# A second buffer for the input block, its squares computed a stage ahead, and two weight slots for three

## The reference

```
u = einsum('ntc,hc->nth', x, W_in)          # x: the normed input
gate, xh = split(u, 2)                      # 1536 channels each
xh = causal_depthwise_conv(xh, conv_w, conv_b)          # 4 taps
forget, inp = split(einsum('nth,gh->ntg', xh, W_gates) + b_gates, 2)
alpha = exp(-8.0 * softplus(forget_base) * sigmoid(forget))
beta = sqrt(1.0 - alpha ** 2 + 1e-06)
h = scan(alpha, beta * sigmoid(inp) * xh)   # h[t] = alpha[t] h[t-1] + xs[t]
out = einsum('nth,dh->ntd', gelu(gate) * h, W_out)
...
x = x + layernorm(attn(layernorm(x)))
x = x + layernorm(ffn(layernorm(x)))        # 8 experts, top 2, and a shared one
```

## Time and profile before

| | us |
|---|---|
| runs shown, lower and higher | 5487.73 and 5763.81 |
| their median | 5625.77 |
| profiled execution, its own time | 5491.87 |
| its span, core 4 | 5490.3 |
| spans of the 8 cores | 5464.4 to 5490.3 |
| attention half (from the start to about) | 2064 |

### The profile page before, as it was taken

One profiled execution on the slowest core, in us unless ns is written; L12 is line 12 of the kernel. 1 busy time (PEld: TensorE's weight loads), 2 busy tenths in 40 slices (PEclk: granted clock), 3 DMA queues, 4 the chain that ended last, 5 costly groups with the idle time before them and its releaser, 6 DMA issues.

```text
span 5490.3 us, 51919 instructions; the slowest of 8 cores (5464.4 to 5490.3 us)
## 1 busy us (share of the span) xinstructions
PE 3922.1 (71%) x15984; PEld 1604.2 (29%) x16304; DVE 2466.9 (45%) x4064; ACT 1187.5 (22%) x1715; POOL 632.0 (12%) x1186
## 2 busy tenths in 40 slices
PE   5566566656464753888888898873688888888883
PEld 1122222212121211333333333330233333333331
DVE  2433433333424245544445544446444554444545
ACT  1342242304132230221111211110111121111220
POOL 1010101111111110111111111110011111111110
PEclk9787788778787875999999999995899999999996
DMA  4454454444353530343333343330233334333341
GB/s 71 61 85 64 64 81 67 66 60 68 47 86 45 81 52 16 56 73 64 62 62 59 62 71 62 62 62 31 39 62 62 59 63 70 63 62 62 58 72 41
DMA packets 179676, 336.65 MB, mean 61 GB/s; under 512 B 19424, under 2 KB 39920, under 8 KB 179280
## 3 DMA queue, kind: packets, MB, share of 16 engines
q0 software_dynamic: 175248, 324.92, 37.5%
q1 hardware_dynamic: 4160, 8.39, 0.4%
HBM read 649.41 MB, written 8.39 MB: 120 GB/s over the span
## 4 chain that ended last, share of the span: by engine, by line
PE 62%; DVE 15%; ACT 11%; DMA 6%; issue 5%; DVEq 1%; ACTq 0%; POOL 0%; another core or an unknown queue 0%; POOLq 0%
PE pb L163 62%; ACT bufA L816 4%; DMA wi<-wi_xh 2%; DMA wi<-wi_gate 2%; DVE sh L469 1%; DVE sa L451 1%; DMA sxbf<-xin 1%; ACT L447 1%; ACT sla L447 1%; ACT L503 1%; DVE sxnbf L366 1%; DVE ssqbf L361 1%; DVE sa L454 1%; DVE st L463 1%; DVE st L466 1%
## 5 line engine op out<-in xcount | busy, mean ns | idle before, releaser
L163 PE MATMUL pb<-xn,wq 128*128 128x512 bf16 x9030 | 2027.7, 379 | 278.5 <-ACT bufA L816 268.3
L163 PEld LDWEIGHTS pb<-xn,wq 128*128 128x128 bf16 x9216 | 881.9, 98 | 1430.0 <-issue 411.4
L163 PE MATMUL pb<-sxh,wg 128*128 128x512 bf16 x2256 | 589.2, 421 | 366.3 <-ACT ssf L503 337.6
L163 PE MATMUL pb<-a_s,w2s 128*128 128x512 bf16 x2258 | 544.5, 401 | 127.6 <-DVE a_s L871 124.9
L816 ACT ACTIVATE bufA<-pb,c_b1g 128x512 f32<-128x512 f32 x256 | 175.9, 687 | 1678.4 <-PE pb L163 1678.4
L821 DVE SCALAR_TENSOR_TENSOR bufA<-pb,c_b3g,bufA 128x512 f32<-128x512 f32 x256 | 192.2, 751 | 674.8 <-ACT bufA L816 674.8
L163 PEld LDWEIGHTS pb<-sxh,wg 128*128 128x128 bf16 x2304 | 237.6, 106 | 717.7 <-issue 519.2
L163 PE MATMUL pb<-sxnbf,wi 128*128 128x512 bf16 x1128 | 303.3, 408 | 145.8 <-DVE sxnbf L366 71.1
L163 PEld LDWEIGHTS pb<-a_s,w2s 128*128 128x128 bf16 x2304 | 231.7, 102 | 432.4 <-issue 196.3
L850 DVE TENSOR_TENSOR bufA<-bufA,bufC 128x512 f32<-128x512 f32 x288 | 199.5, 693 | 241.3 <-ACT bufC L845 241.3
L845 ACT ACTIVATE bufC<-bufA 128x512 f32<-128x512 f32 x288 | 181.2, 629 | 467.3 <-DVE bufA L840 467.2
(11 more groups left out here) (143 smaller groups left out, 2926.0 us busy)
## 6 DMA issues: line engine op xcount, KB each, us to landing
wg<-wgates POOLq DMA_DIRECT2D x192, 384.0 KB, 5.7
wq<-w1g POOLq DMA_DIRECT2D x128, 256.0 KB, 4.1
wq<-w3g POOLq DMA_DIRECT2D x128, 256.0 KB, 4.8
wq<-w1l POOLq DMA_DIRECT2D x128, 256.0 KB, 6.2
wq<-w3l POOLq DMA_DIRECT2D x128, 256.0 KB, 7.0
w2s<-w POOLq DMA_DIRECT2D x128, 256.0 KB, 5.1
wi<-wi_xh POOLq DMA_DIRECT2D x96, 256.0 KB, 4.8
wi<-wi_gate POOLq DMA_DIRECT2D x48, 256.0 KB, 4.8
```

The source lines that it names most:

```text
L163: t.matmul(o, l, r, start=s1, stop=s2),
```

## The change

The input block and its squares get two buffers each, `sxbf2` and `ssqbf2`, used in turn by even and odd stages. Stage 0 loads and squares its own block ahead of the loop. In each stage but the last, behind the normalisation, the next block's load is put into GpSimd's list, ahead of the stage's `wi` loads, and its eight squares into VectorE's list, ahead of the roll and the evictions. The load into a buffer waits for what last read that buffer, two stages back from its own stage. Room is made by dropping `sla`, `st1` and `sh`: the middle part now works in place in `ssf`, `ssi` and `sa2`, and the closing norm in `sao` in place of `ssqbf`. The `wi` stream has two slots where it had three. Counts of instructions of each kind stay as they were.

```diff
-            sxbf = asb("sxbf", [128, NC_D, ST], BF16)
+            sxbf2 = asb("sxbf2", [128, 2, NC_D, ST], BF16)
...
-            ssqbf = asb("ssqbf", [128, NC_D, ST], BF16)
+            ssqbf2 = asb("ssqbf2", [128, 2, NC_D, ST], BF16)
...
-            sla = asb("sla", [128, 2, ST], F32)
...
-            st1 = asb("st1", [128, 2, ST], F32)
-            sh = asb("sh", [128, 2, ST], F32)
...
-            wi = WStream([asb(f"wi{j}", [128, NC_D, 128], BF16) for j in range(3)], "wi", "wi")
+            wi = WStream([asb(f"wi{j}", [128, NC_D, 128], BF16) for j in range(2)], "wi", "wi")
...
+            pre = {}
+            pre[0] = {"xld": g_dma(sxbf2[:, 0], d_x[:, :, 0:ST], sem="x0", tag="x0"),
+                      "xsem": "x0"}
+            sq_v0 = []
+            for c in range(NC_D):
+                v_op(lambda v, c=c: v.tensor_tensor(out=ssqbf2[:, 0, c, :],
...
+            pre[0]["sq_v"] = sq_v0
...
-                lw = [guard["sxbf"]] if "sxbf" in guard else []
-                xld = g_dma(sxbf[:], d_x[:, :, T0:T0 + ST], waits=lw, sem="x",
-                            tag=f"x{st}")
...
-                sqw = [guard["ssqbf"]] if "ssqbf" in guard else []
-                sq_v = []
-                for c in range(NC_D):
...
+                sxbf = sxbf2[:, par]
+                ssqbf = ssqbf2[:, par]
+
+                xld = pre[st]["xld"]
+                sq_v = pre[st]["sq_v"]
+                xw = [(pre[st]["xsem"], xld), ("c", wc)]
...
-                guard["ssqbf"] = ("v", S.n["v"])
                 xn_done = ("v", S.n["v"])
+                guard[("ssqbf", par)] = xn_done
                 if not main:
-                    guard["sxbf"] = xn_done
+                    guard[("sxbf", par)] = xn_done
...
+                if st + 1 < _nst:
+                    np_ = (st + 1) % 2
+                    lw = [g for g in (guard.get(("sxbf", np_)),) if g]
+                    nxld = g_dma(sxbf2[:, np_], d_x[:, :, T0 + ST:T0 + 2 * ST],
+                                 waits=lw, sem=f"x{np_}", tag=f"x{st + 1}")
+                    sqw = [g for g in (guard.get(("ssqbf", np_)),) if g]
+                    nsq = []
+                    for c in range(NC_D):
+                        v_op(lambda v, c=c, np_=np_: v.tensor_tensor(
+                                out=ssqbf2[:, np_, c, :],
...
+                             waits=([(f"x{np_}", nxld)] + sqw) if c == 0 else [],
+                             tag=f"sq{st + 1}")
+                        nsq.append([("v", S.n["v"])])
+                    pre[st + 1] = {"xld": nxld, "sq_v": nsq, "xsem": f"x{np_}"}
...
-                            out=sla[:, pp, :], in0=ssf[:, pp, :],
+                            out=ssf[:, pp, :], in0=ssf[:, pp, :],
...
-                            out=sla[:, pp, :], in_=sla[:, pp, :], func=AF.Exp),
+                            out=ssf[:, pp, :], in_=ssf[:, pp, :], func=AF.Exp),
...
-                            out=sa2[:, pp, :], in0=sla[:, pp, :], in1=sla[:, pp, :],
+                            out=sa2[:, pp, :], in0=ssf[:, pp, :], in1=ssf[:, pp, :],
...
-                            out=st1[:, pp, :], in0=sa2[:, pp, :], in1=ssi[:, pp, :],
+                            out=ssi[:, pp, :], in0=sa2[:, pp, :], in1=ssi[:, pp, :],
...
-                            out=sh[:, pp, :], data0=sla[:, pp, :], data1=st1[:, pp, :],
+                            out=sa2[:, pp, :], data0=ssf[:, pp, :], data1=ssi[:, pp, :],
...
-                                in1=sh[:, pp, :], op=OP.mult),
+                                in1=sa2[:, pp, :], op=OP.mult),
...
+                guard[("ssqbf", par)] = ("t", stats_done)
...
-                            out=ssqbf[:, c, :], in0=sao[:, c, :], in1=pb[6][:, :],
+                            out=sao[:, c, :], in0=sao[:, c, :], in1=pb[6][:, :],
...
-                            out=sao[:, c, :], in0=ssqbf[:, c, :], in1=pb[7][:, :],
+                            out=sao[:, c, :], in0=sao[:, c, :], in1=pb[7][:, :],
...
-                guard["ssqbf"] = ("v", S.n["v"])
...
-                guard["sxbf"] = ("v", S.n["v"])
+                guard[("sxbf", par)] = ("v", S.n["v"])
```

More of the change, by code:

```diff
@@ L333, in build_nc @@
             _nst = int(_os.environ.get("KDBG_NST", NST))
+            pre = {}
[4 more added lines that the diff above has]
+                v_op(lambda v, c=c: v.tensor_tensor(out=ssqbf2[:, 0, c, :],
+                                                    in0=sxbf2[:, 0, c, :],
+                                                    in1=sxbf2[:, 0, c, :], op=OP.mult),
+                     waits=([("x0", pre[0]["xld"])]) if c == 0 else [],
+                     tag="sq0")
+                sq_v0.append([("v", S.n["v"])])
+            pre[0]["sq_v"] = sq_v0
             for st in range(_nst):
@@ L360, in build_nc @@
                 for c in range(NC_D):
-                    v_op(lambda v, c=c: v.tensor_tensor(
+                    v_op(lambda v, c=c, sxbf=sxbf, ssqbf=ssqbf: v.tensor_tensor(
                             out=ssqbf[:, c, :], in0=sxbf[:, c, :],
@@ L365, in build_nc @@
                          tag=f"xna{st}")
-                    v_op(lambda v, c=c: v.tensor_tensor(
+                    v_op(lambda v, c=c, ssqbf=ssqbf: v.tensor_tensor(
                             out=sxnbf[:, c, :], in0=ssqbf[:, c, :],
@@ L370, in build_nc @@
                     xn_v[c] = ("v", S.n["v"])
-                guard["ssqbf"] = ("v", S.n["v"])
                 xn_done = ("v", S.n["v"])
+                guard[("ssqbf", par)] = xn_done
                 if not main:
-                    guard["sxbf"] = xn_done
+                    guard[("sxbf", par)] = xn_done
                 bank_guard[6] = xn_done
                 bank_guard[7] = xn_done
+                if st + 1 < _nst:
[8 more added lines that the diff above has]
+                                out=ssqbf2[:, np_, c, :],
+                                in0=sxbf2[:, np_, c, :],
+                                in1=sxbf2[:, np_, c, :], op=OP.mult),
+                             waits=([(f"x{np_}", nxld)] + sqw) if c == 0 else [],
+                             tag=f"sq{st + 1}")
+                        nsq.append([("v", S.n["v"])])
+                    pre[st + 1] = {"xld": nxld, "sq_v": nsq, "xsem": f"x{np_}"}
                 if st > 0:
@@ L463, in midtail @@
                     v_op(lambda v, pp=pp: v.tensor_tensor(
-                            out=st1[:, pp, :], in0=sa2[:, pp, :], in1=ssi[:, pp, :],
+                            out=ssi[:, pp, :], in0=sa2[:, pp, :], in1=ssi[:, pp, :],
                             op=OP.mult), waits=[beta_done], tag=f"bsi{st}")
                     v_op(lambda v, pp=pp, mi=mi: v.tensor_tensor(
-                            out=st1[:, pp, :], in0=st1[:, pp, :], in1=sxh[:, mi, :],
+                            out=ssi[:, pp, :], in0=ssi[:, pp, :], in1=sxh[:, mi, :],
                             op=OP.mult), tag=f"xs{st}")
                     v_op(lambda v, pp=pp, mi=mi: v.tensor_tensor_scan(
-                            out=sh[:, pp, :], data0=sla[:, pp, :], data1=st1[:, pp, :],
+                            out=sa2[:, pp, :], data0=ssf[:, pp, :], data1=ssi[:, pp, :],
                             initial=hcol[:, mi:mi + 1], op0=OP.mult, op1=OP.add),
@@ L473, in midtail @@
                     v_op(lambda v, pp=pp, mi=mi: v.tensor_copy(
-                            out=hcol[:, mi:mi + 1], in_=sh[:, pp, ST - 1:ST]),
+                            out=hcol[:, mi:mi + 1], in_=sa2[:, pp, ST - 1:ST]),
                          tag=f"hc{st}")
@@ L562, in build_nc @@
                         ao_a = ("a", S.n["a"])
-                        v_op(lambda v, m=m, b=b: v.tensor_tensor(
+                        v_op(lambda v, m=m, b=b, ssqbf=ssqbf: v.tensor_tensor(
                                 out=ssqbf[:, m, :], in0=sxnbf[:, m, :],
@@ L578, in build_nc @@
                     v_op(lambda v, c=c: v.tensor_tensor(
-                            out=sao[:, c, :], in0=ssqbf[:, c, :], in1=pb[7][:, :],
+                            out=sao[:, c, :], in0=sao[:, c, :], in1=pb[7][:, :],
                             op=OP.subtract), tag=f"x1b{st}")
-                    v_op(lambda v, c=c, Tm=Tm: v.tensor_tensor(
+                    v_op(lambda v, c=c, Tm=Tm, sxbf=sxbf: v.tensor_tensor(
                             out=x1[:, c, Tm:Tm + ST], in0=sao[:, c, :],
                             in1=sxbf[:, c, :], op=OP.add), tag=f"x1c{st}")
-                guard["ssqbf"] = ("v", S.n["v"])
                 guard["sao"] = ("v", S.n["v"])
-                guard["sxbf"] = ("v", S.n["v"])
+                guard[("sxbf", par)] = ("v", S.n["v"])
                 bank_guard[6] = ("v", S.n["v"])
```

## The result

The changed kernel is slower by one per cent: the ratio of its time to that of the kernel before is 1.0097, with a 95% interval of 1.0081 to 1.0112. Its executions took 5536.3 to 5544.0 us, those of before 5483.9 to 5491.7. The forecast was 5547; the profiled execution took 5544.4.

A forecast was written before the change was run, and what follows sets the result against it. The prediction took the attention half to be bound by waits for the input block and wi reloads, not matmuls. From 5491.87 us, plus 132.4 for loops, minus 77.3 for entries, it forecast 5547 us, range 5505 to 5620.

The forecast's parts named there:

- Entries of stages 1 to 7: Start of stages 1 to 7: row statistics no longer wait for the input load or its squares; gain 77.3 us.
- Loops: Projection loops with two wi slots: 21.8 us longer with both projections, 11.3 with one; 132.4 us in all.
- The landing time: wi loads in the projection loop: 4.1 us from issue to landing, with 3.7 and 4.84 as ends.
- The 0.9 us for a last load that meets those for `wg`: End of each projection loop: the last wi load meets the wg loads and adds 0.9 us.
- one group per loop go at the lower clock: Projection loop: one matmul group takes 3.4 us for 1.9 at the lower clock, adding 1.5 us per loop.
- rival (a): Projection loop: TensorE falls to the lower clock; 72 us more, giving 5619; chance 0.14.
- the verdict behind the sum: Whole kernel: sum 1.0% slower, but measurement taken to tell only about 2%, so "no change", chance 0.85, leaning to slower.
- The delayed first reload: First wi reload after the normalisation: it gets going only when the squares end; 21 us, giving 5568; chance 0.10.
- Rival (b): wi reload in projection loop gets much shorter with two slots: 5525, by the fit 5463; chance 0.06 as faster than before.
- Rival (c): wi reload in the projection loop is not eased and stays 4.84 us; +41 us, giving 5588; inside the main case's 0.70.
- Rival (d): Stage entries: the guard still waits for the residual adds; losing all of 57.3 us gives 5604; chance within rival (a)'s.
- Where the third group starts: Projection loop: TensorE cannot start its third matmul group before X+5.4 us, X being the end of the normalisation.

The follow-up runs named there:

- two slots alone: The kernel before with two wi slots for three and nothing else; 5599, 5605 and 5607 us, a fourth execution 5682, ratio over all four 1.0244.
- the squares late: The changed kernel with the next stage's squares moved behind the projection loop, ahead of the convolution; 5531.3 us in one execution.
- the two experiments on the squares: The changed kernel with the next stage's squares moved behind the projection loop (5531.3 us), or with each of them computed twice (ratio to before 1.0169).

## Why the prediction was right, and where it was wrong

**The size was right: 5547 us forecast, 5544 measured.** Its two large terms, each found alone by an experiment:

- Entries of stages 1 to 7, 77.3 us forecast. On the slowest cores of the two profiles the distances to the instruction ahead were 5.14 us four times, 22.0, 19.5 and 16.1, and are 0.17 each: 77.0 us. The guard and the queue behaved as worked out, and stage 0 lost nothing (its normalisation ended at 64.4 us before, at 62.5 after).
- Loops, 132.4 us forecast. From the slowest core of one profile to that of the other they are 135 us longer, on the mean of the 8 cores 120. The loops with two projections last 79.6 to 82.3 us on core 7, for 79.9 forecast, the others 37.6 to 41.5, for 39.9.

**That the sum came out within 3 us is in part luck.** Both terms stand for one core each. I read the entries on core 4 alone, and it was the extreme: at stage 5 it waited 22.0 us, core 5 18.7, and the other six 15.1 to 16.5. On the mean of the 8 cores the entries gained 68 us. So against the means both terms were some 10 us too large, and being of opposite sign they cancelled: 120 - 68 = 52 us, and the mean span grew by 48.5. On the two slowest cores 135 - 77 = 58 us stand against the measured 53; the other 5 lie in the rest of the stages, which no experiment looked at.

**Inside the loop term three parts were off and partly cancelled.** The landing time is 3.9 to 4.0 us on the mean, not 4.1: 6 to 11 us too much. The 0.9 us for a last load that meets those for `wg` hardly occurs: that load takes 3.99 us in the loops with two projections and 4.39 in the others (means of 32), about 5 us too much in all. The third part is the clock. I let one group per loop go at the lower clock. Counted by matmuls that start 0.43 us apart in place of 0.21, behind the first two groups, it is on the mean 2.6 groups in a loop with two projections and 0.8 in one with one, against 0.6 and 0.2 before; on core 7 it is 4.2 and 1.4, 22 groups in place of 8. At 1.5 us each this is the part that was sized too small, by up to 21 us on core 7 (an upper end, since not every group lies on the chain). So rival (a) is true in part. Stage 5 of core 7 by stretches, in the columns of the earlier trace rows, and TensorE near its end:

```profile
1198.00:1209.50 11.50, 9.38 (x28) 3.44 (x29) 2.50 (x4) 0.00 (x0) 1.06 (x3) 0.70 0.43 65
1209.50:1230.00 20.50, 11.85 (x52) 4.50 (x51) 4.42 (x7) 0.00 (x0) 3.69 (x7) 1.00 0.59 79
1230.00:1250.00 20.00, 11.97 (x52) 4.36 (x49) 0.69 (x1) 4.37 (x7) 3.17 (x6) 1.00 0.61 88
1250.00:1272.00 22.00, 15.32 (x49) 5.51 (x50) 0.00 (x0) 3.48 (x6) 4.23 (x8) 0.77 0.61 97
...
1251.04 1.89 PE L163 MATMUL pb<-sxnbf,wi 128*128 128x512 bf16 x8 [1.24 <-DMA wi<-wi_gate]
1255.36 2.42 PE L163 MATMUL pb<-sxnbf,wi 128*128 128x512 bf16 x8 [2.43 <-DMA wi<-wi_gate]
1258.90 5.82 PE L163 MATMUL pb<-sxnbf,wi 128*128 128x512 bf16 x16 [1.13 <-DMA wi<-wi_gate]
```

The steady part of the loop, where TensorE is busy 58 to 60% of the time with gaps of 1 to 2 us, keeps 1.00, the 2.4 GHz level: there the rival is refuted. The lower level shows near the loop's start, with a mean of 0.70, and again near its end, here in the group behind a gap of 2.43 us: it takes 2.42 us in place of 1.89. Of the changed kernel's 32 loops with two projections, the 7 with a granted clock of 0.935 or more last 76.1 us on the mean, and the 11 with 0.915 or less last 80.1. The same split gives 75.3 and 79.7 for two slots alone, and 75.9 and 80.0 with the squares late. The kernel's time, which is that of the slowest core, is the time of a core that met this often. It never comes near the 72 us of the rival.

**The step that failed is the verdict behind the sum.** The prediction said: "About 2% is what a measurement of this kernel can tell from no change, so I expect 'no change'". Its own sum was 1.0% slower, and the measurement separates that from nothing with an interval of 0.15% to either side. The mechanism and the sum called for "slower", and I put a bound of 2% above it that no row shows. The two runs shown differed by 5%, but that is not the resolution of executions that are alike. Rows of the profile would have warned: the 8 cores of one execution agreed within 0.5%.

**The delayed first reload (chance 0.10) does not exist here.** The landing times in the two experiments on the squares show no hold-up, with bf16 squares of 425 ns running back to back over the issue and what follows it. The 5.9 us of the earlier trace rows may then have been the queue ahead of that load, as the prediction left open; conversions of that kind were not tried. The Trainium skill, page "SBUF — State Buffer", section "SBUF: two separate sides", warns of this for operations in a mode that holds both ports. What the runs exclude is that these squares are such a case. So the prediction should not have carried that rule over to them.

**Rival (b)**, a much shorter landing, is refuted: of the 1024 `wi` loads that the changed kernel issues behind X the shortest took 3.5 us. The fit of the Trainium skill, page "DMA: Bandwidth & Descriptors", section "Anatomy of one DMA — SWDGE (gpsimd) path", gives an estimate of 2.6; the measurement decides. **Rival (c)**, no easing at all, is refuted too: 4.7 became 3.9 with two slots, and 5.0 with four. **Rival (d)** is refuted by the 0.17 us at every entry.

Where the third group starts was right to 0.3 us: X+5.4 forecast, X+5.7 measured (1198.07 against 1192.34 at stage 5).

## What to carry to other kernels

Where a stream's consumer catches up with its loads, the pace is one slot's round trip (use, release, issue, landing) over the number of slots. Read the round trip from two rows of the chain, divide, and compare with the bare work: 7.4 / 3 = 2.5 against 1.90 us says at once that this loop hangs on its slots. Here the third slot's 2 KB a partition were worth 119 us, and a fourth's 57, against 68 us (the mean of the cores) for all seven entries. Before a slot is given up for another buffer, look for memory that is idle in just that phase, as `sao` was. Read a wait on all 8 cores before it is priced: at one entry it was 22 us on the core shown and 15 to 17 on six others. And hold a forecast's verdict against the interval that executions which are alike allow, not against the widest pair of times at hand.

## What the runs showed that I had not expected

The landing time of a 256 KB load depends mildly on how many are in flight: 3.8 us for a lone one, 3.9 with two slots, 4.7 with three, 5.0 with four, while the rate in the two-projection loops rises from about 80 to 122 GB/s on a core. That is why each further slot still paid. And idle time of TensorE has a second price: 4.2 us of extra wait ahead of the third group made one-projection loops 5.0 us longer, with the granted clock over them at 0.86 in place of 0.90 (cores 4 to 7 of both profiles).
